# Zero matmuls in four waits of TensorE, in a four-block transformer kernel on one core

## The chip, the cores and the metric

The kernel runs on one core of a Trainium2 chip. The metric is the device time of one execution in microseconds. Engines are named as in the profile: PE (TensorE), PEld (its weight loads), DVE (VectorE), ACT (ScalarE), POOL (GpSimd) and SP, which issues DMAs here. PE's clock is granted at one of two levels, 2.4 GHz (1.00 in the rows) and 1.2 GHz (0.50).

## What is computed

The input x is (2, 512, 256): two batches of 512 tokens. Four blocks follow one another, each as x = x + layernorm(block(layernorm(x))). Cut to what matters:

```python
x = L0_attn_h
# 0: causal softmax attention, 16 heads of 128, rotary q and k, own layernorm ahead, residual behind
x = x + _layernorm(_L0_attn_ref(_layernorm(x), ...))
# 1: gate, up and down projections, hidden width 2048, 4-bit weights times block scales
#    inter = gelu(gate) * up; out = inter @ Wd.T
x = x + _layernorm(_L0_ffn_ref(_layernorm(x), ...))
# 2: linear attention by running sums along the tokens, element by element
#    out = q * cumsum(k * v) / (q * cumsum(k) + EPS), q, k = elu(.) + 1, then a projection
x = x + _layernorm(_L1_attn_ref(_layernorm(x), ...))
# 3: gate, up and down again, hidden width 688, weights looked up in a table of 16 values
x = x + _layernorm(_L1_ffn_ref(_layernorm(x), ...))
```

## The kernel before, in words

Every fp32 operand of a matrix product is split into a high and a low fp16 part, and a product is three matmuls (`product`, L1325): high by high, high by low, low by high. Each engine has an order written out by hand, and semaphores join them; `then_inc` counts up behind an instruction, `wait_ge` holds the engine's queue until a count is reached. PE therefore never overtakes a wait. The 8 PSUM banks have roles: two take sums over heads or hidden tiles (`acc_bank`), four hold score rows (`S_bank`, `T_bank`; in the later phases `G_bank` and `U_bank` for gate and up, by parity of the tile), two are for the side work (`proj_bank` and `o_bank`, later `side_bank`).

**Start.** POOL makes constants, among them `identb` and `zerob` (128x512 of zeros). DVE and ACT normalise batch 0. PE runs `keep_warm(4)` (L1347), transposes the first batch (`turn_norm0`, L1337) and runs `keep_warm(1)` (L1349). `keep_warm(n)` is a hardware loop of n rounds with four matmuls of `zerob` by `identb` into `S_bank[1]`, which nobody reads from there. Then PE waits for the low part of the transposed batch (`d_xTl`) and opens the sums (`open_sums`, L1463).

**Attention, block 0.** 32 units (2 batches of 16 heads), in steps from -2 to 33. In PE's `step(s)` stand the scores of unit s, q of unit s+2, v of unit s, the output projection of unit s-2, k of unit s+2 and the weighted sum of unit s-1. `scores` waits for the high parts of q and k (ACT, L669) and the low ones (POOL, L502); POOL first rotates q and k (L494, L495) from what DVE wrote (L986, L988), and between units it makes low parts of weight pieces (L472).

**The later blocks.** Batch 0 runs ahead and batch 1 follows, four runs of hidden tiles on PE: run 1 and 2 are block 1 for batch 0 and 1 (16 tiles each), run 3 and 4 block 3 for batch 0 and 1 (6 tiles each, the last one of 48 rows). A tile is gate (ACT makes gelu or silu, L737), up (DVE multiplies the two, L1162, which counts `d_inter`), the split of the product (ACT L743, POOL L525) and, one tile later, `down` into the sums. Beside the runs stands block 2. For batch 1 ("batch 1's second attention") its projections lie in run 3 (`project1`), DVE makes the running sums and the reciprocal (`denominator`, L1182, and `attend`, L1200), ACT and POOL split the result (L759, L539), and behind run 3 PE multiplies it by the output weights (`out_project1(1)`, L1631, 24 matmuls of 256 columns). In DVE's order of run 3 the last tile's product stands behind `denominator` and `attend`:

```python
for m in range(I_TILES):
    ...
    if m == 5:
        denominator(FT + 1)
        attend(FT + 1)
    product_of(B * M_TILES + m, i_rows(m))
```

Behind `out_project1(1)` PE has the last `down` of run 3 (12 matmuls with 48 rows), while DVE and ACT take the statistics, normalise, add and normalise again (L849, L853, L858, L863, L1094). PE then transposes batch 1 (`turn_norm(3, 1)`, L1476), ACT and DVE split the transposed rows (L724, L1120), and run 4 begins with the gates. Behind run 4 the last norm is made and the output is written.

Of the kernel before, what the change touches and what calls it, by code (L numbers as in the profile page):

```python
# [79 lines left out]
def sandwich(nc, x_in, wqT, wkT, wvT, woT, bqT, bkT, bvT, bo, gT, bT, ropes, w1T, packed, scales, codes, lut, out):  # L80
    with ExitStack() as ctx:
# [3 lines left out]
        def sem(name):  # L85
            return ctx.enter_context(nc.semaphore(name))
# [133 lines left out]
        d_inter = sem("d_inter")  # L220
# [144 lines left out]
        def there(u):  # L365

            return 0 <= u < UNITS
# [952 lines left out]
        def _(pe):  # L1320
# [9 lines left out]
            def turn_norm0(b, cs=range(KC)):  # L1330
                if b:
                    pe.wait_ge(a_nrm0, 1)
                else:
                    pe.wait_ge(d_nrm0, 1)
                for c in cs:
                    for t in range(TPB):
                        last = pe.transpose((proj_bank if b else T_bank[c])[:, t * P:(t + 1) * P], nrm[:, b * TPB + t, c * P:(c + 1) * P],  # L1337
                                            identf[:, :])
                    last.then_inc(t_xT, 1)

            def keep_warm(n):

                with pe.Fori(0, n):
                    for _ in range(4):
                        pe.matmul(S_bank[1][:, :], identb[:, :], zerob[:, :], start=True, stop=True)

            keep_warm(4)  # L1347
            turn_norm0(0)
            keep_warm(1)  # L1349
            pe.wait_ge(d_xTl, KC)  # L1350

            def lows_done(j):
# [7 lines left out]
            def scores(u, q):  # L1360
                b, h, p = head(u)
                if q == 0:
                    pe.wait_ge(a_qkh, 2 * u + 2)
                    pe.wait_ge(g_qkl, 2 * u + 2)
                if u:
                    pe.wait_ge(d_pl, TPB * (u - 1) + q + 1)
                n = (q + 1) * P
                qs = [a[:, p, 0, q * P:(q + 1) * P] for a in (qkh, qkl)]
                ks = [a[:, p, 1, 0:n] for a in (qkh, qkl)]
                product(row_bank[q][:, 0:n], qs, ks, True, False)  # L1370
                pe.matmul(row_bank[q][:, q * P:n], identb[:, :], maskb[:, :], start=False, stop=True).then_inc(t_S, 1)  # L1371

            def project(u, w):
                b, h, p = head(u)
                if u or w:
                    pe.wait_ge(d_rope, 2 * u + w)
                if w == 0 and u - 3 in X0_TURN_AT:
                    pe.wait_ge(d_xT, KC + X0_TURN_AT[u - 3] + 1)
                if h == 0 and w == 0:
                    pe.wait_ge(d_xTl, (b + 1) * KC)  # L1380
                for c in range(KC):
                    if u == 0 and c == 0:
                        pe.wait_ge(d_early, w + 1)
                    if u == EARLY // DK:
                        lows_done(2 * w + c)
                    if u == HEADS // 2:
                        lows_done(FIRST_W + 2 + 2 * w + c)
                    ws = [a[w][:, h * DK + c * HD:(h + 1) * DK + c * HD] for a in (wh, wl)]
                    xs = [a[:, c, b * S:(b + 1) * S] for a in (xTh, xTl)]
                    last = product(proj_bank[:, :], ws, xs, c == 0, c == KC - 1)  # L1390
                last.then_inc(t_proj, 1)

            def project_v(u):
                b, h, p = head(u)
                if u >= 2:
                    pe.wait_ge(d_ol, u - 1)
                if u == 0:
                    pe.wait_ge(d_early, 3)
                if u == EARLY // DK:
                    lows_done(QK_W)  # L1400
                    lows_done(QK_W + 1)
                if u == HEADS // 2:
                    lows_done(FIRST_W + 2 + QK_W)
                    lows_done(FIRST_W + 3 + QK_W)
                for t in range(TPB):
                    for c in range(KC):
                        xs = [a[:, c, b * S + t * P:b * S + (t + 1) * P] for a in (xTh, xTl)]
                        ws = [a[2][:, h * DK + c * HD:(h + 1) * DK + c * HD] for a in (wh, wl)]
                        last = product(o_bank[:, t * P:(t + 1) * P], xs, ws, c == 0, c == KC - 1)
                last.then_inc(t_v, 1)  # L1410

            def weigh(u):
                b, h, p = head(u)
                pe.wait_ge(d_vl, min(u + 2, UNITS))
                for q in range(TPB):
                    pe.wait_ge(s_pT[q], 16 * (u + 1))
                for k in range(TPB):
                    vs = [a[:, p, k * P:(k + 1) * P] for a in (vh, vl)]
                    ps = [pT[:, p, k, i, k * P:S] for i in range(2)]
                    last = product(o_bank[:, k * P:S], vs, ps, k == 0, k == TPB - 1)  # L1420
                last.then_inc(t_pv, 1)
# [11 lines left out]
                last.then_inc(t_op, 1)  # L1433

            def step(s):
                if there(s):
                    for q in range(TPB):
                        scores(s, q)
                if there(s + 2):
                    project(s + 2, 0)  # L1440
                if there(s):
                    project_v(s)
                if s == HEADS + 2:
                    pe.wait_ge(d_acc, 1)
                    open_sums()
                if there(s - 2):
                    out_project(s - 2)
                if there(s + 2):
                    project(s + 2, 1)
                if s in X0_TURN_AT:  # L1450
                    pe.wait_ge(d_rope, 2 * (s + 2) + 2)
                    turn_norm0(1, (X0_TURN_AT[s],))
                if s == UNITS:
                    pe.wait_ge(d_rope, 2 * UNITS)
                    pe.wait_ge(d_pl, TPB * UNITS)
                    turn_norm(1, 0, even_odd)
                if there(s - 1):
                    weigh(s - 1)

            def open_sums():  # L1460

                for a in acc_bank:
                    pe.matmul(a[:, :], identb[:, :], zerob[:, :], start=True, stop=False, skip_group_check=True)  # L1463
# [58 lines left out]
            def out_project1(b):  # L1522
                pe.wait_ge(g_attl, FT * (b + 1))
                for t in range(TPB):
                    for f in range(FT):
                        parts = [a[f][:, t * P:(t + 1) * P] for a in (atth, attl)]
                        ws = [a[:, f, 3 * D:4 * D] for a in (w1h, w1l)]
                        last = product(side_bank[t // 2][:, t % 2 * D:t % 2 * D + D], parts, ws, f == 0, f == FT - 1)
                last.then_inc(t_out1, 1)
# [17 lines left out]
            def down(n, m, before, weights, rows):  # L1547

                r = rows(m)
                if m == 0:  # L1550
                    pe.wait_ge(d_acc, SUMS.index(before) + 1)
                    open_sums()
                pe.wait_ge(g_il, n + 1)
                ws = weights(2, m, 0)
                for t in range(TPB):
                    hs = [a[n % 2][0:r, t * P:(t + 1) * P] for a in (ih, il)]
                    last = product(row_tile(t), hs, ws, False, False, skip=True)
                last.then_inc(t_down, 1)
# [4 lines left out]
            def fp4_weights(b):  # L1563
                def weights(w, m, c):
                    if b == 0 and m % 4 == 0 and c == 0:
                        pe.wait_ge(d_fl, NIBBLES * (m // 4 * 3 + w + 1))
                    if w < 2:
                        return [f[w][:, c, m * P:(m + 1) * P] for f in (fh, fl)]
                    return [f[2][:, m % NIBBLES, m // NIBBLES * D:(m // NIBBLES + 1) * D] for f in (fh, fl)]
                return weights  # L1570
# [39 lines left out]
            run1, run2, run3, run4 = 0, M_TILES, B * M_TILES, B * M_TILES + I_TILES  # L1610
# [14 lines left out]
            for m in range(I_TILES):  # L1625
                gate_up(run3 + m, m, 0, table_weights, i_rows, beside_third)
                if m:
                    down(run3 + m - 1, m - 1, (1, 1), table_weights, i_rows)
                else:
                    down(run3 - 1, M_TILES - 1, None, fp4_weights(1), all_rows)  # L1630
            out_project1(1)  # L1631
            down(run4 - 1, I_TILES - 1, None, table_weights, i_rows)
            pe.wait_ge(d_acc, SUMS.index((2, 1)) + 1)
            turn_norm(3, 1, halves)
            pe.wait_ge(d_xTl, (TURNS.index((3, 1)) + 1) * KC)
# [61 lines left out]
```

## Time and profile before

| | us |
|---|---|
| median of 3 timed runs | 702.58 (702.53 to 702.62) |
| the profiled execution, its own time | 699.39 |
| span of the profiled execution, first to last instruction | 697.6 |
| mean granted clock of PE in it | 0.932 of 2.4 GHz |
| PE busy | 561.1 (80%) |
| DVE busy | 549.6 (79%) |
| ACT busy | 399.6 (57%) |
| POOL busy | 388.6 (56%) |
| PE on the chain that ended last | 39% |
| DVE on it | 29% |

The span is divided into times from the first instruction; the profiled execution's own time is 1.8 us more than its span. The chain that ended last is followed back from the last instruction, at each step to what released it. A duration of a matmul in the rows includes its way through the array, which overlaps the next one; how fast they follow one another is read from their starts.

### The profile page before, as it was taken

Reading aid. Unit: us, or ns where it says so; the run is one execution under the profiler, and the core shown is the slowest. Engines: PE = TensorE matmul, PEld = TensorE weight load, DVE = VectorE, ACT = ScalarE, POOL = GpSimd, SP = SyncE. Lnnn points to the kernel's source line nnn. Section 1 sums busy time; section 2 is a strip of 40 time slices with the busy share of each in tenths; the row PEclk is TensorE's granted clock in tenths of the full one; section 3 lists DMA queues with packets and bytes.
Section 4 is the critical chain, followed back from the end, with each engine's and each line's share of the span. In section 5 each row is a group of like instructions: output and inputs, shape, how many; then the busy total and the mean of one; then the engine's idle time right before and its main releaser. Section 6 shows DMA issues by size and latency. Waiting matters only on the chain.

```text
span 697.6 us, 10855 instructions
## 1 busy us (share of the span) xinstructions
PE 561.1 (80%) x3843; PEld 339.9 (49%) x3848; DVE 549.6 (79%) x1103; ACT 399.6 (57%) x838; POOL 388.6 (56%) x312
## 2 busy tenths in 40 slices
PE   5378788989899999999777787969964968793494
PEld 2145456565566666666543444535532634352252
DVE  6578779878789998998799999887469494667643
ACT  4578667877776687787744344355542345462141
POOL 3698866999988787778456566211442101154021
PEclk8899989999999999999989999989989899997597
DMA  7255443433335485344332130111001010000000
GB/s 257 83 129 126 105 110 81 95 77 68 52 76 74 77 179 90 66 66 75 78 101 76 62 90 1 32 39 34 1 0 46 15 32 1 0 1 0 0 31 30
DMA packets 100741, 44.58 MB, mean 64 GB/s; under 512 B 88272, under 2 KB 93520, under 8 KB 100688
## 3 DMA queue, kind: packets, MB, share of 16 engines
q1 hardware_dynamic: 99696, 43.35, 28.1%
q8 instruction: 30, 0.49, 0.3%
q10 hardware_dynamic: 992, 0.55, 0.3%
q14 instruction: 23, 0.19, 0.1%
HBM read 21.86 MB, written 1.05 MB: 33 GB/s over the span
## 4 chain that ended last, share of the span: by engine, by line
PE 39%; DVE 29%; issue 10%; ACT 9%; POOL 6%; POOLq 0%; DVEq 0%; ACTq 0%
PE bank L1325 34%; PE bank L1501 3%; DVE turned L1153 2%; DVE stage L1182 2%; DVE turned L1162 2%; DVE stats L849 2%; POOL rr L494 1%; POOL rr L495 1%; DVE xT L964 1%; DVE pT L962 1%; DVE y L863 1%; DVE pT L963 1%; DVE pT L971 1%; DVE wql L1114 1%; DVE wkl L1114 1%
## 5 line engine op out<-in xcount | busy, mean ns | idle before, releaser
L525 POOL TENSOR_TENSOR qkl<-turned,qkh 128x512 f16<-128x512 f32 (+1 forms) x44 | 57.4, 1304 | 178.3 <-ACT qkh L743 178.3
L494 POOL TENSOR_TENSOR rr<-turned 64x512 f32<-64x512 f32 x64 | 86.7, 1354 | 12.2 <-DVE turned L988 8.2
L502 POOL TENSOR_TENSOR qkl<-rr,qkh 128x512 f16<-128x512 f32 x64 | 73.8, 1158 | 29.4 <-ACT qkh L669 27.0
L743 ACT ACTIVATE qkh<-turned 128x512 f16<-128x512 f32 (+1 forms) x44 | 27.7, 629 | 108.5 <-DVE turned L1162 108.5
L650 ACT ACTIVATE bank<-bank,nmax 128x128 f32<-128x128 f32 (+3 forms) x128 | 64.1, 501 | 37.8 <-DVE nmax L977 37.3
L495 POOL TENSOR_TENSOR rr<-turned 64x512 f32<-64x512 f32 x64 | 81.9, 1279 | 3.7
L977 DVE TENSOR_REDUCE nmax<-bank 128x1 f32<-128x128 f32 (+3 forms) x128 | 58.2, 484 | 15.0 <-PE bank L1371 13.3
L1162 DVE SCALAR_TENSOR_TENSOR turned<-bank,turned 128x512 f32<-128x512 f32 (+1 forms) x44 | 30.0, 682 | 46.4 <-PE bank L1325 20.8
L999 DVE SCALAR_TENSOR_TENSOR parts<-bank,rscaled,parts 128x128 f16<-128x128 f32 (+3 forms) x128 | 65.8, 547 | 0.3 <-ACT parts L661 0.3
L1325 PE MATMUL bank<-qkh 128*128 128x128 f16 (+3 forms) x128 | 38.9, 304 | 24.7 <-issue 16.3
L661 ACT ACTIVATE parts<-bank,rscaled 128x128 f16<-128x128 f32 (+3 forms) x128 | 57.2, 529 | 1.2 <-DMA pT<-parts 0.2
L1325 PE MATMUL bank<-pT,vh 128*128 128x512 f16 (+3 forms) x256 | 56.6, 311 | 1.5 <-DVE vl L1007 1.2
L1325 PE MATMUL bank<-xTh,wkh 128*128 128x512 f16 x128 | 50.1, 391 | 5.6 <-DVE turned L988 4.4
L1325 PE MATMUL bank<-xTh,wqh 128*128 128x512 f16 x128 | 50.5, 395 | 1.5 <-DVE turned L988 1.5
L1325 PE MATMUL bank<-xTl,wqh 128*128 128x512 f16 x128 | 50.1, 392 | 0.0
L1325 PE MATMUL bank<-xTh,wql 128*128 128x512 f16 x128 | 50.0, 391 | 0.0
L669 ACT ACTIVATE qkh<-rr 128x512 f16<-128x512 f32 x64 | 40.5, 634 | 16.1 <-POOL rr L495 16.1
L1325 PE MATMUL bank<-xTl,wkh 128*128 128x512 f16 x128 | 49.8, 389 | 0.0
L1325 PE MATMUL bank<-xTh,wkl 128*128 128x512 f16 x128 | 49.7, 388 | 0.0
L1325 PE MATMUL bank<-wvh,qkh 128*128 128x256 f16 x128 | 36.3, 284 | 16.3 <-POOL qkl L525 16.3
L1325 PE MATMUL bank<-wvh,xTh 128*128 128x128 f16 x256 | 44.6, 219 | 2.2 <-DVE ol L1013 2.2
L1325 PE MATMUL bank<-wvh,xTl 128*128 128x128 f16 x256 | 44.5, 219 | 0.0
(224 smaller groups left out, 1722.4 us busy)
## 6 DMA issues: line engine op xcount, KB each, us to landing
xa<-in_codes SPq DMA_DIRECT2D x32, 128.0 KB, 2.7
stage<-in_packed SPq DMA_DIRECT2D x12, 256.0 KB, 3.1
stage<-in_scales SPq DMA_DIRECT2D x12, 256.0 KB, 3.7
stage<-in_woT SPq DMA_DIRECT2D x4, 512.0 KB, 3.5
pT<-parts SPq DMA_TRANSPOSE x128, 2.8
x<-in_x SPq DMA_DIRECT2D x2, 512.0 KB, 7.2
stage<-in_wqT SPq DMA_DIRECT2D x2, 512.0 KB, 4.2
stage<-in_wkT SPq DMA_DIRECT2D x2, 512.0 KB, 4.0
```

Of the source, the lines that this page charges most:

```text
L494: pool.tensor_tensor(rr[low, w, :], cos_a[part], sin_b[part], ALU.subtract)
L495: pool.tensor_tensor(rr[high, w, :], cos_b[part], sin_a[part], ALU.add).then_inc(g_rot, 1)
L502: pool.tensor_tensor(qkl[:, p, w, :], rr[:, w, :], qkh[:, p, w, :], ALU.subtract).then_inc(g_qkl, 1)
L525: pool.tensor_tensor(il[n % 2][0:rows, :], inter[0:rows, n % 2, :], ih[n % 2][0:rows, :], ALU.subtract).then_inc(g_il, 1)
L650: act.activation(row, row, ACT.Exp, bias=nmax[:, p, q:q + 1], accum_out=psum_row[:, p, q:q + 1]).then_inc(a_exp, 1)
L661: act.activation(row_parts[q][:, :, 0, :], row_bank[q][:, 0:(q + 1) * P].rearrange("p (k n) -> p k n", n=P), ACT.Copy, scale=rscaled[:, p, ...
L669: act.activation(qkh[:, p, w, :], rr[:, w, :], ACT.Copy).then_inc(a_qkh, 1)
L743: act.activation(ih[n % 2][0:rows, :], inter[0:rows, n % 2, :], ACT.Copy).then_inc(a_ih, 1)
L977: dve.tensor_reduce(nmax[:, p, q:q + 1], row_bank[q][:, 0:(q + 1) * P], AX_X, ALU.max, negate=True).then_inc(d_max, 1)
L999: dve.scalar_tensor_tensor(out=row_parts[q][:, :, 1, :], in0=row_bank[q][:, 0:(q + 1) * P].rearrange("p (k n) -> p k n", n=P), scalar=rsca ...
L1162: dve.scalar_tensor_tensor(out=inter[0:rows, n % 2, :], in0=U_bank[n % 2][0:rows, :], scalar=1 / (X_SCALE * W_SCALE), in1=gel[0:rows, n % ...
L1325: last = pe.matmul(dst, l, r, start=start and i == 0, stop=stop and i == 2, skip_group_check=skip)
```

## The change

PE gets more of the zero matmuls. The second `keep_warm` goes from 1 round to 4. A `keep_warm(4)` stands ahead of the scores of unit 0. Behind run 3 PE waits until DVE has made all 38 products of the first three runs (`d_inter` at `run4`, which is 38), runs `keep_warm(5)`, then `out_project1(1)` and the last `down` as before, and `keep_warm(7)` ahead of the wait for the transposes. The bank written is `S_bank[1]`, which is also the gate bank of the odd tiles; the new wait sees to it that tile 37 has been read.

```diff
             keep_warm(4)
             turn_norm0(0)
-            keep_warm(1)
+            keep_warm(4)
             pe.wait_ge(d_xTl, KC)
...
             def step(s):
+                if s == 0:
+                    keep_warm(4)
                 if there(s):
                     for q in range(TPB):
                         scores(s, q)
...
+            pe.wait_ge(d_inter, run4)
+            keep_warm(5)
             out_project1(1)
             down(run4 - 1, I_TILES - 1, None, table_weights, i_rows)
+            keep_warm(7)
             pe.wait_ge(d_acc, SUMS.index((2, 1)) + 1)
             turn_norm(3, 1, halves)
```

## Rows read from the trace of the kernel before

**Rows 1.** The page: PE's granted clock in 40 equal slices, in tenths.

```profile
PEclk8899989999999999999989999989989899997597
```

**Rows 2.** PE's timeline, 0 to 46 us: start, us, operation, count, [idle before <-releaser].

```profile
2.97 5.10 PE L1345 MATMUL bank<-zerob,identb 128*128 128x512 bf16 x16 [2.97 <-POOL maskb L465]
8.57 1.09 PE L1337 MATMUL bank<-identf,nrm 128*128 128x128 f32 x8 [0.50 <-DVE nrm L901]
9.50 1.03 PE L1345 MATMUL bank<-zerob,identb 128*128 128x512 bf16 x4
15.44 1.03 PE L1463 MATMUL bank<-zerob,identb 128*128 128x512 bf16 x2 [4.91 <-DVE xTl L929]
...
34.04 0.26 PE L1325 MATMUL bank<-qkh 128*128 128x128 f16 x1 [5.01 <-POOL qkl L502]
...
37.19 0.38 PE L1325 MATMUL bank<-xTh,wqh 128*128 128x512 f16 x1
...
44.97 0.22 PE L1325 MATMUL bank<-qkh 128*128 128x128 f16 x1 [3.35 <-POOL qkl L502]
```

**Rows 3.** Timelines of DVE, ACT and POOL, 0 to 60 us.

```profile
17.35 1.39 DVE L889 BATCH_NORM_STATS2 stats<-x 128x6 f32<-128x256 f32 x4
...
19.16 0.75 DVE L986 SCALAR_TENSOR_TENSOR turned<-bank,bias_q,rope 128x512 f32<-128x512 f32 x1
...
39.89 0.63 ACT L669 ACTIVATE qkh<-rr 128x512 f16<-128x512 f32 x1 [0.99 <-POOL rr L495]
...
33.85 3.24 POOL L472 TENSOR_TENSOR wvl<-stage,wvh 128x768 f16<-128x768 f32 x2
...
45.09 2.17 POOL L494 TENSOR_TENSOR rr<-turned 64x512 f32<-64x512 f32 x1 [0.22 <-DVE turned L988]
```

**Rows 4.** Stretches: us, busy time by engine, PE's granted clock (PEclk), DMA.

```profile
33.00:34.00 1.00, 0.00 (x0) 0.00 (x0) 0.00 (x0) 1.00 (x2) 1.00 (x2) 0.67 0.00 0
36.00:37.00 1.00, 1.00 (x6) 0.48 (x4) 0.53 (x1) 0.43 (x2) 1.00 (x1) 0.63 0.26 70
44.00:45.00 1.00, 0.03 (x1) 0.06 (x2) 1.00 (x3) 0.37 (x1) 0.87 (x1) 1.00 0.41 83
642.00:644.00 2.00, 0.78 (x4) 0.58 (x5) 0.00 (x0) 1.80 (x2) 1.99 (x2) 0.50 0.02 4
647.00:648.00 1.00, 1.00 (x8) 0.68 (x5) 0.00 (x0) 0.00 (x0) 0.00 (x0) 0.64 0.00 0
650.00:652.00 2.00, 0.00 (x0) 0.00 (x0) 1.60 (x6) 0.30 (x1) 0.00 (x0) 0.79 0.00 0
658.00:660.00 2.00, 1.67 (x8) 1.27 (x6) 1.40 (x4) 0.89 (x2) 0.00 (x0) 0.50 0.00 0
```

**Rows 5.** PE's timeline, 626 to 666 us.

```profile
643.22 0.40 PE L1325 MATMUL bank<-w1h,parts 128*128 128x256 f16 x1 [6.41 <-POOL parts L539]
...
648.13 0.28 PE L1325 MATMUL bank<-w2dh,qkh 48*128 48x256 f16 x1
...
657.73 1.94 PE L1476 MATMUL bank<-identf,nrm 128*128 128x128 f32 x8 [8.12 <-issue]
...
664.85 0.38 PE L1325 MATMUL bank<-xTh,woh 128*128 128x512 f16 x1
```

**Rows 6.** DVE's timeline, 620 to 698 us.

```profile
641.18 0.68 DVE L1162 SCALAR_TENSOR_TENSOR turned<-bank,turned 48x512 f32<-48x512 f32 x1
```

**Rows 7.** The chain that ended last, in order of time, 610 to 698 us.

```profile
643.22 4.99 PE bank L1325 x24
...
648.23 1.44 DVE stats L849 x4
...
661.09 7.17 PE bank L1325 x24
```

**Rows 8.** The same chain, 0 to 60 us.

```profile
46.98 2.65 PE bank L1325 x30
...
54.65 2.14 POOL wol L472
```

## The prediction

> **What bounds the kernel now.** I read the page first: PE's granted clock is not at full level in every slice, and the lowest ones lie near the end [rows 1]. So the question is where PE runs at 1.2 GHz while the end of the kernel waits for it, and four views answer it: PE's timeline around each edit, the other engines' timelines beside it, the chain that ended last, and the granted clock in short stretches.
>
> Prices come first. The opening warm loop issues 16 matmuls of 512 columns in 5.10 us [rows 2], some at either level; the four of the second loop take 1.03 us with the drain of the last [rows 2], so 0.216 us each at 2.4 GHz. In the last part nine matmuls of 512 columns lie between 661.09 and 664.85 [rows 5, 7], 0.42 us each, at 1.2 GHz. The first loop also shows that multiplying zeros does bring the clock up, and that a loop adds no gap worth pricing: seven matmuls at 0.427 and nine at 0.216 make 4.93 us, and the drain the rest of the 5.10.
>
> **Edit 1, the second warm loop from 4 to 16 matmuls.** They run from 9.50 to about 13.0, inside the 4.91 us in which PE waits for xTl until 15.44 [rows 2], so they delay nothing. If the clock is then up at 15.44, the first projection ends up to 1.7 us before its 19.03. Its reader is DVE's L986, which started at 19.16 straight behind DVE's own statistics of 17.35 [rows 3]; DVE was late, not PE. Worth 0; what hides it is DVE's work, and PE was only 0.1 us from being late too, so a cost would need a slower projection, which nothing here brings.
>
> **Edit 2, 16 matmuls ahead of the first scores.** PE stands idle 5.01 us until 34.04 for qkl, and runs the 16 score matmuls in 3.15 us (34.04 to 37.19), at 0.50 until some point between 36 and 37 [rows 2, 4]. The loop fits: 28.9 plus 16 x 0.216 is 32.3. The scores' 4,352 columns at 2.4 GHz take 1.85 us, so PE gains 1.3 us. Who uses it? Next on the way is ACT's qkh at 39.89, which waited 0.99 us for POOL's rotation, and POOL was working through its weight pieces from 33.85 and through rotations behind them; its next gap, at 45.09, is 0.22 us [rows 3]. POOL sets the time here, whatever PE does. Gain 0.
>
> It has a cost behind it. The second unit's scores wait for POOL's qkl and start at 44.97, now after 3.35 us of idle PE, and at full clock [rows 2, 4]. With the first scores, the projection and V 1.3 us earlier, the projection that ended the stretch finishes at about 40.2, and the gap grows to about 4.8 us. A gap of 3.35 us was survived; in the gap of 5.01 us ahead of 34.04 the clock had fallen within the slice 33 to 34 [rows 4]. So I expect the fall. These scores are on the chain: PE from 44.97 to 49.63, then ACT, then POOL's wol at 54.65 [rows 8]. All of them at 1.2 GHz cost 3.63 - 1.85 = 1.8 us, none cost 0, and the first scores paid 1.3. I take the middle, **+0.9 us**.
>
> **Edit 3, a wait and 20 matmuls ahead of out_project1(1).** PE's wait there looks 6.41 us long, to 643.22 [rows 5]. But the new wait asks for the last product of the third run, and DVE makes it only at 641.18 to 641.86, since the step's denominator and attend stand before it in DVE's order [rows 6]. So the loop cannot begin before 641.9, and 1.3 us of the wait are left for it. It begins at 0.50 [rows 4]. The clock rose 2.7 us after the first matmul of a burst at 34.04, 3.8 us after that of 661.09, and in the slice 647 to 648, some 4.5 us after that of 643.22 [rows 2, 4, 5, 7]. Cold for 2.5 to 4.5 us, the loop takes 20 x 0.216 = 4.3 us plus half of the cold time, 5.6 to 6.6 us. It ends at 647.5 to 648.5, where out_project1 was almost done before. At 2.4 GHz its 24 matmuls of 256 columns then take 24 x 0.109 = 2.6 us instead of 4.99 [rows 7], ending at 650.2 to 651.2, against 648.21. DVE's statistics started 0.02 us behind that end [rows 7] and ACT, DVE and PE follow one another, so the delay is whole. Ends of the range: even a loop all at 2.4 GHz gives 641.9 + 4.3 + 2.6 = 648.8, +0.6 us; a late rise gives +3.0. I take **+2.1 us**, nearer the lower end of the cold times, since the loop starts 1.3 us sooner than the burst that had to wait 4.5. Nothing on DVE or ACT is queued behind the new wait itself; it only holds PE, whose next work is the projection and the down step behind it.
>
> **Edit 4, 28 matmuls behind the down step.** From the end of out_project1 to the transposes lie 9.52 us of DVE and ACT [rows 5, 7]. The down step takes 1.3 of it, 28 x 0.216 = 6.05 us follow, and 2.2 us of idle remain: no delay, if the clock is up, which edit 3 sees to. (Wholly at 1.2 GHz the loop would take 12 us and be 3.7 late.) Before, the clock fell in the slice 650 to 652, and the eight transposes took 1.94 us at 0.50 against 1.09 in the row at 8.57 [rows 2, 4, 5]. Now they run fast: some 0.7 us earlier gates, as ACT and DVE have to follow. Then come the gates at 661.09, whose nine cold matmuls cost 9 x 0.21 = 1.8 us over full clock, and PE is on the chain from there on [rows 5, 7]. Whether the clock holds that far is the open point: from the loop's end to the gates are 2.2 us idle, 1.1 of transposes and 1.5 idle, 4.8 us with nothing but transposes. In the slice 658 to 660 PE did hardly anything but the transposes, for 1.67 us, and stayed at 0.50; the rise came only with the gates, at 664.85 [rows 4, 5]. So I let it fall, later than before; the gates are cold for 2.5 to 3 instead of 3.8 us, 0.5 us gained. Together **-1.2 us**; ends -0.7 (transposes alone) and -2.5 (clock held).
>
> By the Trainium skill ("TensorE: Matmul & The Clock Gate", Part 4) transposes do not count as busy for the clock as other matmuls do. The trace agrees as far as the slice 658 to 660 shows; by that rule the sum stays as above.
>
> **Sum:** 0 + 0.9 + 2.1 - 1.2 = +1.8 us. The profiled execution took 699.39 us for its span of 697.6; it would take 701.2. The three timed runs lie 3.2 us higher, at 702.58; I add the 1.8 to them: **704.4 us**. About 1.4 us (0.2%) is what can be told from no change here.
>
> **Rivals.**
> 1. *The costs cancel* (0.36). The clock survives the gap ahead of 44.97 or POOL absorbs the delay (0), and edit 3 comes early to full clock (+1.6 to +2.0) against edit 4's -1.2 to -1.6: 0 to +0.8. For it: 3.35 us were survived, and 4.8 is not far beyond 4.5. 703.0.
> 2. *Faster* (0.07): the clock holds from the long loop to the gates, -2.5 us, which brings the whole last run to full clock, and the scores' 1.3 us do pass on. With +2.0 for edit 3 it makes -1.8, 700.8. It decides at the 4.8 us with the transposes in them; it needs these to keep the clock up, against the slice 658 to 660, and a way round POOL at 37 to 45, against its gapless row. The hold without the early gain makes -0.4, which falls under rival 1.
> 3. *The cold stretches fall otherwise than in the profiled execution* (0.15). If the clock's changes do not lie at fixed places in the kernel, both kernels pay other cold stretches. Edit 3 has at the least 0.6 and, with a late rise, 3.0 to cost; a late rise with the clock lost again ahead of the gates gives 0.9 + 3.0 - 0.7 = +3.2, 705.8. The three runs agree within 0.09 us, which speaks against much wandering; the 3.2 us between them and the profiled one speak for different places. The Trainium skill ("TensorE: Matmul & The Clock Gate", Part 1) says that the number of cold matmuls changes from run to run for this reason; this trace is a single execution and cannot show it.
> 4. *The change does not do what it says*: for edit 3 this is part of the forecast, as 1.3 of 6.4 us of its wait are left.
>
> **How the numbers follow.** Forecast 0.42, cancel 0.36, late rise 0.15, faster 0.07. The forecast's own range is +1.0 to +2.8, a tenth of its cases under 1.4; late rise is wholly slower. Slower by over 0.2%: 0.42 x 0.9 + 0.15 + a little of the cancelling case = 0.55; faster 0.07; within 0.2%: 0.38. The range leaves out the faster case and the top of the late rise: -0.6 to +3.6, 702.0 to 706.2.
>
> **What would show it.** In the profile after: DVE L986 still at 19.16 and POOL's L494 still at 45.09; the matmuls at 44.97 at 0.50 (edit 2 right) or at 1.00 (its cost is 0); the 20 zero matmuls starting within 0.1 us of DVE's last L1162 and out_project1 starting 4 us or more later than before, at full clock; the transposes at 1.09 us; the clock at the first gates, 0.50 for the forecast, 1.00 for rival 2. The forecast is wrong if out_project1 ends less than 0.6 us later than before relative to that L1162, or if a gain of PE ahead of 40 us reaches POOL.

## The result

The changed kernel takes 703.57 us (median of 22 runs, 701.52 to 706.99), the kernel before 701.02 us (22 runs, 697.71 to 702.62). The ratio is 1.0041, with a 95% interval of 1.0030 to 1.0053: **slower by 0.41%, 2.9 us** (the two medians themselves lie 2.6 us apart). The forecast was 704.4 us, +1.8 us, with slower by over 0.2% as the likeliest case. The kernel before has a lower median over 22 runs than over the three shown ahead of the prediction.

The profiled execution of the changed kernel took 704.12 us with a span of 702.3, against 699.39 and 697.6. These two single executions differ by 4.7 us, more than the medians do, and part of this section is about why.

The page of the changed kernel, PE's busy time and its granted clock in 40 slices:

```profile
PE 575.2 (82%) x3924; PEld 346.4 (49%) x3924; DVE 549.1 (78%) x1103; ACT 399.6 (57%) x838; POOL 388.4 (55%) x312
...
PEclk9889989999999999999989999989989899996998
```

PE is busier (561.1 us before) and its mean clock higher, 0.944 after 0.932. Its lowest slice, a 5 near the end [rows 1], has become a 6. The kernel is slower all the same.

PE's timeline of the changed kernel, 0 to 46 us, beside [rows 2]:

```profile
9.45 3.62 PE L1345 MATMUL bank<-zerob,identb 128*128 128x512 bf16 x16
15.48 0.61 PE L1465 MATMUL bank<-zerob,identb 128*128 128x512 bf16 x2 [2.42 <-DVE xTl L929]
...
20.55 0.61 PE L1325 MATMUL bank<-xTh,wkh 128*128 128x512 f16 x1 [2.34 <-DVE turned L988]
...
29.08 3.62 PE L1345 MATMUL bank<-zerob,identb 128*128 128x512 bf16 x16
34.10 0.22 PE L1325 MATMUL bank<-qkh 128*128 128x128 f16 x1 [1.40 <-POOL qkl L502]
...
38.91 0.39 PE L1325 MATMUL bank<-xTh,wkh 128*128 128x512 f16 x1 [0.17 <-DVE turned L988]
...
45.01 0.27 PE L1325 MATMUL bank<-qkh 128*128 128x128 f16 x1 [4.63 <-POOL qkl L502]
```

Both early loops fit into their waits: 2.42 and 1.40 us of idle are left behind them. The first scores start at 34.10 as before and run fast, and the stretch of matmuls that ended at about 41.6 before now ends at about 40.4. Ahead of the second unit's scores the idle time is 4.63 us, where it was 3.35.

Stretches of the changed kernel (busy time by engine, then the granted clock, in the columns of [rows 4]):

```profile
43.00:44.00 1.00, 0.00 (x0) 0.00 (x0) 1.00 (x3) 1.00 (x2) 1.00 (x2) 0.86 0.31 66
44.00:45.00 1.00, 0.00 (x0) 0.02 (x1) 1.00 (x3) 0.42 (x1) 0.91 (x1) 0.50 0.36 71
49.00:50.00 1.00, 1.00 (x4) 0.42 (x3) 0.52 (x1) 0.45 (x1) 0.96 (x1) 0.50 0.84 283
50.00:51.00 1.00, 1.00 (x7) 0.41 (x6) 0.00 (x0) 0.85 (x3) 0.98 (x1) 0.72 0.44 172
644.00:645.00 1.00, 0.00 (x0) 0.00 (x0) 0.99 (x2) 0.26 (x1) 0.00 (x0) 0.50 0.00 0
650.00:651.00 1.00, 1.00 (x4) 0.37 (x3) 0.00 (x0) 0.00 (x0) 0.00 (x0) 0.50 0.00 0
651.00:652.00 1.00, 1.00 (x6) 0.39 (x5) 0.00 (x0) 0.00 (x0) 0.00 (x0) 0.85 0.00 0
...
666.00:667.00 1.00, 0.00 (x0) 0.00 (x0) 0.86 (x3) 0.98 (x3) 0.00 (x0) 1.00 0.00 0
667.00:668.00 1.00, 0.37 (x2) 0.21 (x3) 0.57 (x1) 0.98 (x1) 0.00 (x0) 1.00 0.00 0
```

The clock fell in the slice 43 to 44, a little over a microsecond ahead of the scores, and came back only in the slice 50 to 51, at about 50.6. Between 45.01 and there PE's work took about twice its time.

POOL's timeline of the changed kernel, the fifth and the seventh L494 (the rotations of units 2 and 3), which were at 45.09 [rows 3] and 56.94 before:

```profile
45.14 2.17 POOL L494 TENSOR_TENSOR rr<-turned 64x512 f32<-64x512 f32 x1 [0.23 <-DVE turned L988]
...
59.68 1.26 POOL L494 TENSOR_TENSOR rr<-turned 64x512 f32<-64x512 f32 x1 [0.17 <-POOL wol L472]
```

The first stands where it stood. The second is 2.74 us later. Lining up all 64 of these POOL instructions in the two traces shows +0.05 us up to the sixth, +2.7 from the seventh on, and no other jump over 0.35 us up to the last, at +2.3.

The end of run 3, PE's and DVE's timelines of the changed kernel, beside [rows 5, 6]:

```profile
645.42 7.36 PE L1345 MATMUL bank<-zerob,identb 128*128 128x512 bf16 x20 [5.28 <-DVE turned L1162]
652.62 0.27 PE L1325 MATMUL bank<-w1h,parts 128*128 128x256 f16 x1
...
656.75 6.22 PE L1345 MATMUL bank<-zerob,identb 128*128 128x512 bf16 x28
664.92 1.06 PE L1478 MATMUL bank<-identf,nrm 128*128 128x128 f32 x8 [1.96 <-issue]
667.63 0.39 PE L1325 MATMUL bank<-xTh,woh 128*128 128x512 f16 x1 [1.64 <-DVE xTl L1120]
```

```profile
644.62 0.68 DVE L1162 SCALAR_TENSOR_TENSOR turned<-bank,turned 48x512 f32<-48x512 f32 x1
655.44 1.42 DVE L849 BATCH_NORM_STATS2 stats<-bank 128x6 f32<-128x256 f32 x4 [10.14 <-PE bank L1325]
...
689.22 0.68 DVE L1162 SCALAR_TENSOR_TENSOR turned<-bank,turned 48x512 f32<-48x512 f32 x1 [3.32 <-PE bank L1325]
```

DVE's last product of run 3 starts at 644.62, so the kernel is 3.44 us behind here. The 20 zero matmuls start 0.12 us behind its end and take 7.20 us; `out_project1` starts at 652.62, and the statistics behind it stand 10.82 us behind the product, where they stood 7.05 behind it. That is +3.77 us. From the statistics to the first gate it is 12.19 us instead of 12.86 (-0.67), with transposes of 1.06 us, and from the first gate to the last product of run 4 it is 21.59 us instead of 23.40 (-1.81), because the clock held up to the gates and through them. The chain in its order of time shows it:

```profile
667.63 5.35 PE bank L1325 x24
```

The first 24 matmuls of run 4 take 5.35 us where they took 7.17 [rows 7]. The sum of the two traces is 3.44 + 3.77 - 0.67 - 1.81 = +4.73 us, the whole difference of the spans.

Part of this sum belongs to no edit. Of the 3.44 us, 2.3 were there at POOL's last L494. The other 1.1 came between it and DVE's last product of run 3, in code that is the same in both kernels: 307.11 us before, 308.23 in the changed kernel. The clock fell at other places there: at 572.6 in the kernel before and not in the changed one, and at about 589.9 in the changed one and not in the kernel before. The same piece of work in the two, first before, then changed (2.2 us later):

```profile
588.00:589.00 1.00, 1.00 (x12) 0.93 (x11) 0.20 (x1) 0.82 (x2) 0.00 (x0) 1.00 0.00 0
```

```profile
590.00:591.00 1.00, 1.00 (x7) 1.00 (x6) 0.00 (x0) 0.25 (x1) 0.00 (x0) 0.50 0.00 0
```

From the last L494 to that product the twelve profiles of the experiments take between 305.8 and 308.9 us, though nothing that they add stands between the two. Two profiled executions can thus differ by some 3 us for no edit's sake.

### The profile page after: what moved, and what is told of

Same layout as the page of the kernel before. It is cut to its first block and busy times, and to the rows that moved or that the text cites. A ratio compares the mean times of both kernels' runs of the same rounds, so it can differ in the third digit from the quotient of the medians.

```text
span 702.3 us, 11053 instructions
## 1 busy us (share of the span) xinstructions
PE 575.2 (82%) x3924; PEld 346.4 (49%) x3924; DVE 549.1 (78%) x1103; ACT 399.6 (57%) x838; POOL 388.4 (55%) x312
## 5 line engine op out<-in xcount | busy, mean ns | idle before, releaser
L494 POOL TENSOR_TENSOR rr<-turned 64x512 f32<-64x512 f32 x64 | 86.6, 1352 | 12.3 <-DVE turned L988 8.2
```

The source lines that it names most:

```text
L494: pool.tensor_tensor(rr[low, w, :], cos_a[part], sin_b[part], ALU.subtract)
```

## The experiments

Each was timed beside the kernel before on the same chip. Three distances are read from the profiles: from POOL's fifth to its seventh L494 (the early stretch), from DVE's last product of run 3 to the statistics (edit 3's place), and from there to the last product of run 4 (edit 4's place). None of these needs the spans to be compared. The times and ratios come from all timed runs, and where they and the one profiled execution differ, the text says so; the ratio is not the quotient of the two medians.

### Edits 1 and 2 alone

```diff
-            keep_warm(1)
+            keep_warm(4)
...
+                if s == 0:
+                    keep_warm(4)
```

> Edits 1 and 2 alone. Theory A (the first scores' gain is of no use, and the longer idle stretch ahead of the second unit's scores lets the clock fall, which POOL then hands on): slower by 1.5 to 2.7 us, ratio 1.002 to 1.004; the second unit's scores at 0.50 and POOL's seventh L494 1.5 to 3 us later than the 56.9 us of before. Theory B (the early edits do nothing, the loss is all behind run 3): ratio 1.000, POOL's L494 within 0.3 us.

Measured: ratio 0.9992 (0.9976 to 1.0007), 700.84 us against 701.63. Its profile has the expected picture, with 14.31 us from the fifth to the seventh L494 against 11.85 in the profile of before. The time does not show it. Theory A is right about the mechanism in this execution and wrong about what it costs on the average: the interval leaves at most 0.5 us. Theory B's ratio fits and its POOL rows do not. Edit 2 was not timed without edit 1.

### Edit 3 alone

```diff
+            pe.wait_ge(d_inter, run4)
+            keep_warm(5)
             out_project1(1)
```

> Edit 3 alone. Theory A (the loop stands behind DVE's last product and pushes out_project1 back by more than the clock gives back): slower by 2 to 4 us, ratio 1.003 to 1.006; from the start of DVE's last L1162 of run 3 to the statistics L849 some 10 to 11 us instead of 7.05. Theory B (the projection's full clock pays the loop back): ratio 0.999 to 1.001 and that distance 7 to 7.6 us.

Measured: ratio 1.0039 (1.0026 to 1.0052), 704.28 us. Theory A. Its timelines of PE (of the 20 records of the loop some are missing) and DVE:

```profile
644.34 1.49 PE L1345 MATMUL bank<-zerob,identb 128*128 128x512 bf16 x3 [5.57 <-DVE turned L1162]
646.05 1.49 PE L1345 MATMUL bank<-zerob,identb 128*128 128x512 bf16 x3 [0.22 <-issue]
647.75 2.88 PE L1345 MATMUL bank<-zerob,identb 128*128 128x512 bf16 x9 [0.22 <-issue]
```

```profile
643.16 0.68 DVE L1162 SCALAR_TENSOR_TENSOR turned<-bank,turned 48x512 f32<-48x512 f32 x1
653.29 1.43 DVE L849 BATCH_NORM_STATS2 stats<-bank 128x6 f32<-128x256 f32 x4 [9.45 <-PE bank L1325]
```

The first record shown stands 0.5 us behind the product's end, but one ahead of it is missing: counted back from 650.47, with the clock's return at about 648.4, 20 matmuls begin at about 643.9, right behind the product. The loop was cold for some 4.5 us; the distance from product to statistics is 10.13 us.

This profile also explains the run before it. It has neither edit 1 nor 2, and yet POOL's seventh L494 is late:

```profile
45.15 2.17 POOL L494 TENSOR_TENSOR rr<-turned 64x512 f32<-64x512 f32 x1 [0.24 <-DVE turned L988]
...
58.28 1.26 POOL L494 TENSOR_TENSOR rr<-turned 64x512 f32<-64x512 f32 x1 [0.17 <-POOL wol L472]
```

The distance is 13.13 us, not 11.85. The other profiles of kernels that are as before up to here say the same (edit 4 alone 13.32, and of the kernels below 13.34, 13.31 and 13.49). The kernel before mostly pays at this place as well; its profiled execution was the exception. In the five others the idle time ahead of the scores is 2.76 to 3.00 us, shorter than the 3.35 that kept the clock, and the clock fell between 0.7 us ahead of the scores' start and 0.8 us behind it, so that PE had begun to multiply in four of the five. PE's timeline and two stretches of edit 4 alone, whose early part is that of the kernel before:

```profile
45.08 0.22 PE L1325 MATMUL bank<-qkh 128*128 128x128 f16 x1 [2.76 <-POOL qkl L502]
```

```profile
45.00:46.00 1.00, 0.93 (x9) 0.80 (x10) 1.00 (x2) 0.00 (x0) 0.59 (x1) 0.81 0.58 117
46.00:47.00 1.00, 1.00 (x5) 0.56 (x4) 0.99 (x3) 0.31 (x2) 1.00 (x1) 0.50 1.94 145
```

So the length of the gap alone does not decide it.

### Edit 4 alone

```diff
             down(run4 - 1, I_TILES - 1, None, table_weights, i_rows)
+            keep_warm(7)
```

> Edit 4 alone. Theory A (the loop holds the clock through the transposes and often to the gates): faster by 1 to 2.5 us, ratio 0.9965 to 0.9985; transposes in 1.06 to 1.09 us, and from L849's start behind out_project1 to the first gate 12.2 us instead of 12.86. Theory B (the clock is lost again in any case, and the loop, starting behind a cold projection, ends late): ratio 0.999 to 1.002.

Measured: ratio 0.9991 (0.9978 to 1.0004), 700.60 us. In its profile all of theory A is there: transposes of 1.06 us, 12.19 us from the statistics to the gate, 21.59 from there to the last product. Its ratio is theory B's: on the average the gain is about a quarter of that execution's 2.5 us, and at most 1.5 us by the interval. The profiled execution was the fastest of the twelve timed (698.20 of 698.20 to 702.81), so it says little about the others. What can happen in them is shown below.

### Edits 1 and 2, with zeros ahead of the second unit's scores

The sums over heads are open in their bank at this point, and zeros added to them change nothing. So PE can multiply zeros there without a bank of its own.

```diff
+            def add_zeros(n):
+                with pe.Fori(0, n):
+                    for _ in range(4):
+                        pe.matmul(acc_bank[0][:, :], identb[:, :], zerob[:, :], start=False, stop=False, skip_group_check=True)
...
+                if s == 1:
+                    add_zeros(5)
```

> Edits 1 and 2, and 20 further zero matmuls ahead of the second unit's scores, added into the open sums (zeros add nothing). Theory A: they keep the clock up over the idle stretch, so the loss of the early edits goes away: ratio 0.998 to 1.001, POOL's seventh L494 at 56.9 us within 0.3, the scores at 1.00. If the early loss had another cause than that stretch, the ratio stays that of edits 1 and 2 alone.

Measured: ratio 0.9951 (0.9936 to 0.9967), 698.67 us: faster than the kernel before, by more than theory A foresaw. PE's and POOL's timelines:

```profile
40.24 4.26 PE L1351 MATMUL bank<-zerob,identb 128*128 128x512 bf16 x15
44.82 0.22 PE L1325 MATMUL bank<-qkh 128*128 128x128 f16 x1 [0.32 <-issue]
```

```profile
44.94 2.17 POOL L494 TENSOR_TENSOR rr<-turned 64x512 f32<-64x512 f32 x1 [0.22 <-DVE turned L988]
...
56.80 1.26 POOL L494 TENSOR_TENSOR rr<-turned 64x512 f32<-64x512 f32 x1 [0.17 <-POOL wol L472]
```

The scores run at full clock, and the seventh L494 stands 11.86 us behind the fifth. The early time is lost around the gap ahead of these scores, and it is lost in the kernel before as well, which is why filling it gains instead of breaking even.

### Zeros ahead of the second unit's scores, none of the four edits

```diff
+                if s == 1:
+                    add_zeros(3)
```

> None of the four edits; 12 zero matmuls added into the open sums ahead of the second unit's scores. If that stretch is where the early time is lost, in the kernel before too (its profiled execution was a lucky one there), this is faster by 2 to 3 us, ratio 0.996 to 0.997, with POOL's seventh L494 some 11.9 us behind the fifth. If the 0.4% between the two early kernels came from edit 2's warm first scores as well, this gives clearly less: 0.998 to 1.000.

Measured: ratio 0.9961 (0.9946 to 0.9975), 698.63 us, and 11.86 us between the two L494. As expected. Edits 1 and 2 add nothing to it that can be told. The rows hold only part of the gain, though: 11.86 us instead of 13.13 to 13.49 is 1.3 to 1.6 us, and the timed gain is 2.7 us (the interval begins at 1.8). Where the rest comes from, no row here shows.

### Edit 3's loop without its wait

```diff
+            add_zeros(5)
             out_project1(1)
```

> Edit 3 with its 20 zero matmuls put where PE has the time: behind the down step, added into the open sums, with no wait for DVE's product, so they run at about 637 to 643 and not at 642 to 649. Theory A (only the place of the loop makes edit 3 slow): faster by 1.0 to 2.4 us, ratio 0.9965 to 0.9985, from the start of DVE's last product of run 3 to the statistics 4.8 to 6 us. Rival (the loop itself or the fetch behind it costs): 1.000 or slower.

Measured: ratio 0.9990 (0.9974 to 1.0006), 700.62 us. PE's timeline:

```profile
639.91 5.85 PE L1351 MATMUL bank<-zerob,identb 128*128 128x512 bf16 x20
646.52 0.28 PE L1325 MATMUL bank<-w1h,parts 128*128 128x256 f16 x1 [0.77 <-POOL parts L539]
...
658.84 1.94 PE L1482 MATMUL bank<-identf,nrm 128*128 128x128 f32 x8 [8.11 <-issue]
```

The loop starts behind the down step, at 639.91, and ends 0.77 us ahead of the projection, which is held by POOL alone and runs at full clock. The distance from product to statistics is 4.87 us. So the loop costs nothing here and gains some 2 us at its place in this execution. The timed gain of 0.1%, 0.7 us, is less than that and lies in neither theory's range; the interval reaches from 1.8 us faster to 0.4 slower. The row at 658.84 shows that the clock is lost again before the transposes, and the gates, cold now for 4.4 us, have 23.74 us up to the last product against 23.40. That accounts for 0.3 of the missing 1.5 us; the rest is open. The loop writes another bank here than in edit 3, which no run separates from its place.

### Edit 4 with four zero matmuls behind the transposes

```diff
+            keep_warm(7)
             pe.wait_ge(d_acc, SUMS.index((2, 1)) + 1)
             turn_norm(3, 1, halves)
+            keep_warm(1)
```

> Edit 4 and four further zero matmuls between the transposes and the gates. If edit 4 alone was worth only 0.1% because the clock is still often lost over the transposes, this is faster by 1.8 to 2.5 us, ratio 0.9965 to 0.9975; if its gain is spent elsewhere, it stays at 0.999.

Measured: ratio 0.9964 (0.9950 to 0.9979), 698.45 us. As expected: four matmuls turn 0.1% into 0.36%. Only the timed runs show it; in the two profiled executions the clock held either way, and from the statistics to the last product of run 4 both take 33.8 us. So the stretch that edit 4 leaves between its loop and the gates is, as far as the times tell, where its gain is lost in many executions.

### The three together

Zeros ahead of the second unit's scores (3 rounds), edit 3's loop without its wait, and edit 4 with four matmuls behind the transposes, each as in its diff above.

> The three together: zeros ahead of the second unit's scores, the loop of edit 3 without the wait, edit 4 with four matmuls behind the transposes. If the gains add up: faster by 5 to 7 us, ratio 0.990 to 0.993.

Measured: ratio 0.9930 (0.9906 to 0.9955), 696.01 us. Within that interval the gains add up (0.39, 0.10 and 0.36% by themselves). Its profile still lost the clock in the slice 657 to 658, when the four matmuls had just begun at 657.35, and paid 22.49 us instead of 21.59 behind the gate. Four matmuls there do not always hold the clock.

### The changed kernel without edit 3

```diff
-            pe.wait_ge(d_inter, run4)
-            keep_warm(5)
```

> The changed kernel with edit 3 alone undone. If edit 3 carries the whole loss (0.4% by itself) and edits 1, 2 and 4 are worth 0 to 0.2% together: ratio 0.9975 to 0.9990. If the edits' effects do not add up, for instance because edit 4 needs edit 3's warm projection, it is 1.000 or more.

Measured: ratio 0.9993 (0.9977 to 1.0009), 699.98 us, just above the first range. Against the changed kernel's 1.0041 edit 3 is worth 0.48%, 3.4 us; the other three edits together gain nothing that can be told from none.

### The changed kernel with edit 3's loop moved

```diff
-            pe.wait_ge(d_inter, run4)
-            keep_warm(5)
+            add_zeros(5)
             out_project1(1)
```

> The changed kernel with edit 3's loop writing zeros into the open sums instead, without the wait, so that it starts as soon as the down step ends. If the place is what makes edit 3 slow: 0.5% below the changed kernel's 1.0041, ratio 0.996 to 0.999, with out_project1 starting some 2 us behind DVE's last product of run 3 (8.0 us in the changed kernel's profile).

Measured: ratio 0.9977 (0.9966 to 0.9988), 699.43 us. The same 20 matmuls, which cost 0.48% behind the wait, cost nothing where PE is idle, and the whole kernel is now faster than the one before. Whether they gain something themselves is not told: without them it was 0.9993, and the intervals overlap. PE's timeline, and stretches of this kernel:

```profile
638.72 5.97 PE L1351 MATMUL bank<-zerob,identb 128*128 128x512 bf16 x20
645.34 0.28 PE L1325 MATMUL bank<-w1h,parts 128*128 128x256 f16 x1 [0.65 <-POOL parts L539]
```

```profile
656.00:657.00 1.00, 0.00 (x0) 0.00 (x0) 0.96 (x4) 0.00 (x0) 0.00 (x0) 1.00 0.00 0
658.00:659.00 1.00, 0.72 (x7) 0.48 (x5) 0.88 (x3) 0.68 (x2) 0.00 (x0) 0.89 0.00 0
659.00:660.00 1.00, 0.00 (x0) 0.00 (x0) 0.98 (x2) 0.98 (x2) 0.00 (x0) 0.50 0.00 0
...
665.00:666.00 1.00, 1.00 (x5) 0.43 (x4) 0.24 (x1) 0.00 (x0) 0.00 (x0) 0.69 0.00 0
```

`out_project1` starts 2.03 us behind the product's start. The stretches show one of the executions in which edit 4 fails: the clock is at full level until the transposes are done and falls at about 658.8. The gates start at 660.36 and run cold until about 665.6, and it takes 24.17 us to the last product. That is 2.6 us more than with the clock held, and 0.8 more than in the kernel before, which eats what the fast transposes gave.

### Edit 3's wait alone

```diff
+            pe.wait_ge(d_inter, run4)
             out_project1(1)
```

> Edit 3's wait alone, no loop. The wait ends 1.3 us before out_project1 may start anyway, so it costs nothing: ratio 0.999 to 1.001, distance from DVE's last product to the statistics 6.4 to 7.4 us as without it. If the wait itself were the cost: 1.003 or more.

Measured: ratio 1.0004 (0.9990 to 1.0017), 701.07 us, 6.34 us from product to statistics. The wait costs nothing by itself; it costs by what stands behind it.

### A version that beats both

The three together, with 8 rounds instead of 7 behind the down step:

```diff
+                if s == 1:
+                    add_zeros(3)
...
+            add_zeros(5)
             out_project1(1)
             down(run4 - 1, I_TILES - 1, None, table_weights, i_rows)
+            keep_warm(8)
             pe.wait_ge(d_acc, SUMS.index((2, 1)) + 1)
             turn_norm(3, 1, halves)
+            keep_warm(1)
```

> The best of the kernels so far (zeros ahead of the second unit's scores, the loop without the wait ahead of out_project1(1), zeros around the transposes) with 8 rounds instead of 7 behind the down step, so that less idle time stands ahead of the transposes. If the clock's loss over the transposes, seen in that kernel's profile, comes from that idle time: ratio 0.990 to 0.992. If 7 rounds were enough: 0.993 as before. Should the loop end late, the transposes start more than 9.6 us behind the statistics.

Measured: ratio 0.9918 (0.9906 to 0.9931), 694.91 us (5 runs, 694.67 to 695.56). PE's timeline:

```profile
647.08 7.08 PE L1345 MATMUL bank<-zerob,identb 128*128 128x512 bf16 x32
655.25 1.06 PE L1484 MATMUL bank<-identf,nrm 128*128 128x128 f32 x8 [1.10 <-issue]
656.16 1.03 PE L1345 MATMUL bank<-zerob,identb 128*128 128x512 bf16 x4
657.96 0.39 PE L1325 MATMUL bank<-xTh,woh 128*128 128x512 f16 x1 [0.78 <-DVE xTl L1120]
```

1.10 us are left ahead of the transposes and 0.78 ahead of the gates, the distance from statistics to transposes is still 9.48 us, and the last product stands 21.59 us behind the gate. Whether the eighth round itself brings anything is not settled by the two intervals, which overlap.

## Why the prediction was right, and where its sizes were off

The sign and the main cause held. By its steps:

- **Edit 1, 0.** L986 started at 19.12 instead of 19.16, as foreseen. "A slower projection, which nothing here brings" was wrong for the projection behind it, though. The clock, up when the first one began, fell within it at about 16.4 and was still low when k of the first unit began (the matmul at 20.55 takes 0.61 us), where before it had come back by then (0.39), and k was late by 1.2 us for DVE. POOL was at its weight pieces, and its first L494 came at +0.05.
- **Edit 2, gain 0, cost +0.9.** The gain of 1.3 us on the first scores reached nobody, as argued from POOL's row. The mechanism of the cost is there step by step: earlier end, longer idle stretch, fall of the clock, cold scores on the chain. Its size was missed twice. In the pair of profiled executions it is +2.7 us, since the cold stretch went on to 50.6 and took in a projection besides the scores. In the timed runs of edits 1 and 2 it is not there: -0.6 us, at most +0.5, since the kernel before mostly pays at the same place. The step that failed is "a gap of 3.35 us was survived": it was survived in the one execution that was profiled.
- **Edit 3, +2.1 (ends +0.6 and +3.0).** Measured +3.77 in the pair of profiles; timed +2.7 us alone (0.39%) and +3.4 as the part undone (0.48%). The start of the loop behind DVE's product, the place of the loss and the rest of the step are as predicted. The term that was mis-sized is the cold time: 5.9 us in the changed kernel (645.42 to about 651.3) and about 4.5 in edit 3 alone, where I took the rise times of other bursts, 2.5 to 4.5, and leaned to their lower end.
- **Edit 4, -1.2 (ends -0.7 and -2.5).** In the profiles of the changed kernel and of edit 4 alone the clock held and the gain was -2.5, the far end. Timed alone it is -0.6 us (0.09%, not told from none). "I let it fall" describes some executions: the gap with nothing but transposes lost the clock in the kernel with the loop moved, and four matmuls put into it gave 0.27% more. But when it fell there, the gates were cold for 5.3 us, not the 2.5 to 3 of the forecast, and the edit was worth nothing: 36.36 us from the statistics to the last product of run 4, against 36.26 before.
- **The sum** of +1.8 us against +2.9 misses by 1.1 us, about as much as edit 3's step (+2.1 against +3.4 as the part undone). That the other three came out close, -0.3 forecast and -0.5 timed together (0.9993), is luck in part: edit 2's cost is not found in the timed runs, and edit 4 alone gave half of its -1.2, so the two misses cancel. Of the rivals, that the cold stretches fall otherwise than in the profiled execution is what happened, in both kernels. The Trainium skill ("TensorE: Matmul & The Clock Gate", Part 1) has this as a number of cold matmuls that changes from run to run; here the distance between the two L494 was 11.85 us in one profile of a kernel unchanged up to there and 13.13 to 13.49 in five others. My argument against it, three runs within 0.09 us, was weak: 22 runs of the same kernel spread over 4.9 us.

Open: whether edit 2 costs something on the average. The four profiles with it and no zeros behind it have 13.26 to 14.54 us between the two L494, the five above 13.13 to 13.49 and the kernel before 11.85; by their means that would be 0.7 to 1.0 us, and the timed 0.9992, with 0.5 us as its upper end, does not show it.

## What to carry to other kernels

Fill a wait of TensorE only from where it really begins: a wait that the filler itself needs can eat the wait that was to be filled, and what is left behind it delays the work. A loop of zeros must end ahead of its deadline even if it starts cold, and filling one gap is worth little if the next gap loses the clock again. A single profile shows the clock of one execution; before a cold or warm stretch goes into a sum, look whether a second profile of the same code has it too. Nor does the length of a gap tell by itself: 3.35 us kept the clock once, and behind 2.76 us it fell three times.

## What was not expected of the hardware

- After an idle stretch the clock came back as late as 5.9 us after the first matmul of an unbroken burst (645.42 to about 651.3), and 5.5 at the second unit's scores, against 2.7 at 34.04 before.
- The clock can fall while PE multiplies: 0.9 us after the first matmul of 15.48 in the changed kernel (at about 16.4), and 0.5 us after that of 45.08 in edit 4 alone (0.81 in the slice 45 to 46, with PE busy for 0.93 of it).
- A gap of 4.5 to 4.7 us with only the eight transposes in it kept the clock in three profiles (the changed kernel, edit 4 alone, the changed kernel without edit 3) and lost it in the one with the loop moved. By the Trainium skill (the same page, "TensorE: Matmul & The Clock Gate", Part 4) transposes do not count as busy as other matmuls do; these profiles do not decide it, since the same gap went both ways.
- Zeros added into an open accumulation bank keep the clock: with 12 of them the second unit's scores ran at full clock, 11.86 us between the two L494.
